# A Perceiver block on one core: key and value projections contract over 128 rows, 30 of them zero

## What is computed

```python
x = x + L0_xattn(layernorm(x), ctx)   # 4 heads, top 32 of 6272 scores, FiLM, S4D by FFT, MLP
x = x + L0_attn(layernorm(x))         # gated global mix, cumsum, 3-tap convolution
x = x + L0_ffn(layernorm(x))          # 8 experts, top 2, one shared
x = x + L1_xattn(layernorm(x), ctx)   # 16 heads of 8, softmax over 6272
x = x + L1_attn(layernorm(x))         # causal, 16 heads
x = x + L1_ffn(layernorm(x))          # 8 experts, top 2
# L1_xattn:
kh = (kv @ Wk + bk)...                # the key projection of this case
vh = (kv @ Wv + bv)...                # the value projection of this case
```

## Time and profile before

| | |
|---|---|
| median of 3 runs | 322.18 us (321.97 to 328.8) |
| the profiled execution | 320.57 us |
| its span, first to last instruction | 318.8 us |
| mean granted TensorE clock | 0.855 |
| TensorE busy | 244.7 us (77%) |
| VectorE busy | 195.1 us (61%) |
| ScalarE busy | 146.7 us (46%) |
| GpSimd busy | 66.1 us (21%) |

### The profile page before, as it was taken

How to read it: one execution, slowest core, us unless ns; L and a number is a source line. 1 busy time by engine, 2 the same in 40 slices (tenths; PEclk the granted TensorE clock), 3 DMA queues, 4 the chain that set the end, 5 groups by cost and what they waited for, 6 DMA issues and landing times.

```text
span 318.8 us, 5155 instructions
## 1 busy us (share of the span) xinstructions
PE 244.7 (77%) x2021; PEld 149.7 (47%) x2042; DVE 195.1 (61%) x482; ACT 146.7 (46%) x234; POOL 66.1 (21%) x97
## 2 busy tenths in 40 slices
PE   1995852596998658959777988998998888784884
PEld 1342312485873323424554855665665556431422
DVE  3299997898925464435236567776776770224464
ACT  1788930883623425235236575465565556301030
POOL 4895897002000442430013000000000000000000
PEclk9999595776999575558999999999999999757599
DMA  7992001000077000000089999999999509000000
GB/s 203 281 384 93 1 0 31 38 2 0 2 296 296 0 0 0 0 3 0 2 105 124 101 131 122 107 122 123 105 109 120 59 19 373 9 0 0 0 2 4
DMA packets 3807, 26.84 MB, mean 84 GB/s; under 512 B 1212, under 2 KB 1405, under 8 KB 2184
## 3 DMA queue, kind: packets, MB, share of 16 engines
q1 hardware_dynamic: 3784, 26.52, 42.1%
HBM read 16.85 MB, written 0.03 MB: 53 GB/s over the span
## 4 chain that ended last, share of the span: by engine, by line
PE 31%; DVE 9%; issue 5%; ACT 4%; POOL 1%; DVEq 0%; POOLq 0%; ACTq 0%
PE B L1039 17%; PE A L1039 12%; DVE mx L930 3%; ACT probs L606 1%; PE B L1337 1%; ACT mid L597 1%; DVE moe_w L927 1%; ACT moe_w L588 0%; ACT L606 0%; DVE m L969 0%; DVE probs L970 0%; DVE s L973 0%; POOL ctxn L434 0%; POOL ctxn L436 0%; DVE probs L962 0%
## 5 line engine op out<-in xcount | busy, mean ns | idle before, releaser
L930 DVE TENSOR_REDUCE mx<-B 128x1 f32<-128x512 f32 (+1 forms) x104 | 65.1, 656 | 26.2 <-PE B L1039 22.1
L606 ACT ACTIVATE probs<-A 128x896 f32<-128x896 f32 x56 | 51.3, 918 | 37.1 <-PE A L1039 36.8
L343 POOL TENSOR_TENSOR rstd<-ve,mhalf 64x1 f32<-64x1 f32 x10 | 5.5, 546 | 206.0 <-DVE ve L639 204.6
L1039 PE MATMUL B<-probs,scores 128*32 128x128 f32 x736 | 34.0, 280 | 4.9 <-ACT mid L597 3.5
L1039 PE MATMUL A<-ctxT,qq 98*128 98x512 f32 (+1 forms) x52 | 27.4, 690 | 5.4 <-ACT scores L464 4.9
L1039 PE MATMUL B<-scores,moe_w 128*128 128x512 bf16 (+2 forms) x118 | 29.2, 344 | 2.7 <-DVE mx L930 1.0
L1039 PEld LDWEIGHTS B<-probs,scores 128*32 128x32 f32 x736 | 19.2, 109 | 11.4 <-ACT probs L606 6.7
L673 DVE MAX8 mid<-scores 128x8 f32<-128x128 f32 x98 | 19.4, 279 | 4.5 <-ACT scores L464 4.5
L1039 PE MATMUL A<-ctxT,blob_l 98*128 98x512 f32 (+1 forms) x26 | 19.4, 879 | 3.4 <-DVE probs L779 3.4
L1039 PEld LDWEIGHTS A<-ctxT,qq 98*128 98x128 f32 x52 | 11.5, 232 | 21.8 <-issue 11.4
L1039 PE MATMUL A<-moe_w 112*128 112x128 bf16 (+2 forms) x146 | 19.8, 281 | 0.8 <-DVE moe_w L927 0.7
(11 more groups left out here) (347 smaller groups left out, 395.0 us busy)
## 6 DMA issues: line engine op xcount, KB each, us to landing
ctxT<-scores SPq DMA_DIRECT2D x20, 196.0 KB, 7.3
ctxn<-in_ctxn SPq DMA_DIRECT2D x1, 2352.0 KB, 8.2
moe_w<-in_moe_w SPq DMA_DIRECT2D x1, 2304.0 KB, 8.2
ctxn<-in_moe_w SPq DMA_DIRECT2D x1, 2304.0 KB, 9.0
scores<-in_e_gu SPq DMA_DIRECT2D x1, 2048.0 KB, 8.5
ctxn<-scores SPq DMA_DIRECT2D x10, 196.0 KB, 7.3
moe_w<-scores SPq DMA_DIRECT2D x10, 196.0 KB, 6.9
ctxT<-in_ctxT SPq DMA_DIRECT2D x3, 588.0 KB
```

The source lines that it names most:

```text
L343: nc.gpsimd.tensor_tensor(rstd[:, :], ve[:, :], mhalf[0:T, :], ALU.pow).then_inc(S["rstd_ready"], 1)
L606: A_(probs[:, (n % RING) * 1024:(n % RING) * 1024 + w], A[:, 2 * (n % 2):2 * (n % 2) + 2, :].rearrange("p a b -> p (a b)")[:, 0:w], ACT.Ex ...
L930: V.tensor_reduce(mx[:, m, t:t + 1], bank[:, 0:SB0[t][1]], AX_X, ALU.max).then_inc(S["max_used"], 1)
L1039: return mm(out_, lhsT, rhs, start=start, stop=stop)
```

## The change

The transposed context and both weights are used with all 128 rows. Rows 98 to 127 of `ctxT` are loaded as zeros from a new array `pad` (30 x 6272 float32, 735 KB), after `blob_l` and ahead of the wait for the mask rows. `wk1` and `wv1` get 30 rows of zeros on the host; `blob_l` keeps its size. TensorE waits for the new load once, ahead of the first key projection. The scores of the first block still use 98 rows. TensorE's order, its number of matmuls and their columns stay; the other engines' programs stay too.

```diff
-          "wq1": (D, D), "rep_q": (P, KS), "wv1": (KA, V_ROW), "bq1": (D, 1), "scale1": (P, 1), "wo1": (P, D),
-          "mask_hs": (P, 2), "mask_m": (P, NP), "sel_o": (P, 4 * 9), "wk1": (KA, D), "wqT2": (D, D), "wkT2": (D, D), "wvT2": (D, D), "woT2": (D, D),
+          "wq1": (D, D), "rep_q": (P, KS), "wv1": (P, V_ROW), "bq1": (D, 1), "scale1": (P, 1), "wo1": (P, D),
+          "mask_hs": (P, 2), "mask_m": (P, NP), "sel_o": (P, 4 * 9), "wk1": (P, D), "wqT2": (D, D), "wkT2": (D, D), "wvT2": (D, D), "woT2": (D, D),
...
             sp.dma_start(blob["blob_l"][:, :], dram["blob_l"]).then_inc(S["ld_l"], 16)
+            sp.dma_start(ctxT[KA:P, :], dram["pad"]).then_inc(S["ld_pad"], 16)
             sp.wait_ge(S["mask_row"], 4)
             sp.dma_start(ctxn[:, :], dram["ctxn"]).then_inc(S["ld_ctx"], 16)
...
-                    last = one(v_bank(b)[:, i * V_ROW:(i + 1) * V_ROW], chunk_cols(ctxT[0:KA, :], c), W["wv1"])
+                    last = one(v_bank(b)[:, i * V_ROW:(i + 1) * V_ROW], chunk_cols(ctxT, c), W["wv1"])
...
-                    one(A[:, n % 2, 0:w], W["wk1"], ctxT[0:KA, s:s + w]).then_inc(S["k_ps"], 1)
+                    one(A[:, n % 2, 0:w], W["wk1"], ctxT[:, s:s + w]).then_inc(S["k_ps"], 1)
...
             pe.wait_ge(S["ld_l"], 16)
+            pe.wait_ge(S["ld_pad"], 16)
             project_keys("film")
...
+    for n in ("wk1", "wv1"):
+        w[n] = np.concatenate([w[n], np.zeros((P - KA, w[n].shape[1]), np.float32)], 0)
...
+    out["pad"] = np.zeros((P - KA, G), np.float32)
```

More of the change, by code:

```diff
@@ L97 @@
 tokT_ps tokT_sb norm_ready k_ps k_hi k_rest k_mid k_low
-ld_a ld_s ld_m ld_l ld_rows ld_gmask ld_tmask ld_ctx ld_dft ld_w1 ld_w2 ld_gu ld_down out_stored
+ld_a ld_s ld_m ld_l ld_pad ld_rows ld_gmask ld_tmask ld_ctx ld_dft ld_w1 ld_w2 ld_gu ld_down out_stored
 ones_ready var_ready rstd_ready mask_row
```

## The result

The changed kernel took 314.25 us in the median of 4 executions (310.82 to 317.66), the kernel before 322.25 beside it: ratio 0.967 (95% interval 0.961 to 0.973), 8.0 us faster. The forecast was 319.2, with a range of 316.4 to 323.3: the sign was right, the size was not, and the time lies outside the range. The ratios and their intervals leave out every execution more than 1.5% above the fastest of its kernel, so that 0.967 rests on the changed kernel's executions at 310.82 and 312.41 us alone; the medians are over all executions, and their ratio is 0.975.

The account below looks back on a forecast made before the run. The prediction took a serial chain with TensorE at half clock as the bound. Gains of 0.9, 1.95 and 0.2 summed to 3.05, taken as 3.0 us off 322.18: 319.2 us, range 316.4 to 323.3.

Parts of the forecast that it names:

- What bounds the kernel: From 104.9 to 145.8 us: a serial one-block chain with key projections, TensorE doing 29.5 us of work at half clock.
- The mechanism: Matmuls count for the clock by rows contracted: 64 too few, 98 marginal, 128 best; zeros should not matter.
- The first rival, nothing happens: Rows do not count for the clock, or zero rows add nothing: time 322.2 us, chance 0.27.
- The load: Zero rows loaded ahead of `ctxn` make it land 2.6 us later, before its first read: 0 on the path.
- The bound of 21 us: Even at eight times the load's estimated price, `ctxn` would land before it is read.
- First stretch: No clock fall at 104.9 us, so the eight `hT` matmuls at 106.84 run at full clock: gain 0.9 us.
- The bound of 3.1: Upper bound in us for the first stretch, if all of 106.84 to 113.1 ran at full clock.
- Second stretch and behind it: Projections from 124.43 us raise the clock near 128.8, gaining 1.95; router work before the expert matmuls gains 0.2.
- the median moves by the same: Whole kernel: the median, 1.6 us above the profiled execution, drops by the same gain, to 319.2 us.
- rival of a fall in the expert stage: The clock falls near 154 us among the experts instead, costing 3 us: 324.2 us, chance 0.10.

Follow-up runs that it names:

- load_only: Kernel before plus the load of the zero rows and the wait for it, all projections still over 98 rows: 322.72 us, ratio 0.998.
- after_tail_fill: Changed kernel plus two matmuls of ones where TensorE waits right behind the main loop: 312.23 us, ratio 0.973.
- after_again: Changed kernel without any edit, executed six more times: median 318.20 us, from 310.3 to 321.9.
- pad_random: Changed kernel with random numbers instead of zeros in the context's 30 added rows, the weights' added rows still zero: 320.82 us, ratio 0.989.
- before_tail_fill: Kernel before, projections over 98 rows, plus two matmuls of ones right behind the main loop: 316.63 us, ratio 0.983.
- before_delay: Kernel before plus one unused GpSimd operation of 1.1 us between value projections and main loop: 324.47 us, ratio 0.997.

## Why the prediction was right and wrong

**What bounds the kernel: right.** The chain with the key projections at half clock was the place, and TensorE's clock was the lever: the first expert matmul moved 4.3 us forward (forecast: from 140.85 to near 138, measured 136.53; 0.6 of it lies ahead of the chain), and each microsecond behind it moved with it up to the loop's end (4.2 us).

**The mechanism: right, its rule too coarse.** Keys alone carry the chain's gain, values and load none; bursts of 64 rows stayed slow and bursts of 96 and more rose. Calling 98 rows marginal was fair: their bursts rose, and the longest piece over 98 rows rose in none of six profiles. But 128 rows were not better than 98 or 112 in the bursts, only in the kernel, and there 112 rows did in the first stretch what 128 do and in the longest piece no more than 98; the order by rows that the prediction assumed is shown for this piece, and nothing here shows where it comes from. Filled with zeros or with random numbers, the padded rows gave chains of 40.8 and 40.7 us, so zeros count, as argued from the mostly zero operands.

**The first rival, nothing happens: fell.** The times (0.967 at first, 0.980 for the keys alone) and the clock of the stretch (0.70 against 0.50) exclude it. The Trainium skill, page "TensorE: Matmul & The Clock Gate", section "What's actually happening", goes by how busy the array is; bursts of 17.43 us without a gap over 32, 64 and 80 rows stayed at half clock here, so in these runs the measurement decides against that rule as it stands, while the rule in its table at the end, that few rows take the time of many, holds at equal clock: 17.43 us three times.

**The load: no cost, as forecast, at a wrong price.** The estimate by bytes was 2.6 us more until `ctxn` lands after its issue; it was 4.6, and 8.0 in load_only, with the pad itself landing 19.6 and 23.1 us after issue. The price did not go by bytes. The bound of 21 us covered it.

**First stretch: half the size.** Forecast 0.9, measured 1.7 (first key projection to `ut`, 25.1 to 23.4 us). `hT` gave the 0.87 it should. What the sum left out is how far the later fall reaches: it came at 107.7, so the projection behind `hT` still ran in part at full clock (1.50 us for 2.02), and the projection at 117.52 began at full clock, ahead of the fall at 117.9 (1.72 for 2.07). The clock was back at 111.1, not 115.1, and the four projection instructions at 111.12 took 1.98 us instead of 2.99, but that gave nothing: the wait for VectorE behind them grew from 3.41 to 4.42. The bound of 3.1 held.

**Second stretch and behind it: right.** Forecast 1.95 to the end of `glob` and 0.2 behind it, measured 2.1 (132.70 became 128.26, with `ut` at 121.47 and 119.17) and -0.1. The rise came at 124.7, 2.6 us into the projections of 122.13, a little sooner than the 3 to 5.6 taken from other rises (in after_tail_fill the six took 5.51 us, with a rise only at their end), and VectorE's step became the limit ahead of the last two projections (the wait of 0.22 us), as the sum allowed for; the clock fell again at 131.6, before the experts. Sum of the chain: 3.7 instead of 3.05. By this execution alone, 316.08 for the 317.6 that was forecast for its like, and 0.6 of the difference is the earlier start of the chain.

**The step that failed: "the median moves by the same".** The sum took everything behind the expert stage as fixed, with one time. It is not: the tail from the loop's end takes 45 us or 39.3, and the experts and values 1 to 3 us more in some executions. In the kernel before, the fall behind the loop was in the one profile, and the narrow lower end of its 55 executions (none under 319.65) suggests that a tail without it hardly occurs; the changed kernel had it in one of two profiles, and four of its ten executions took 312.41 or less, where a chain 3.7 us shorter than in a profile of 320.57 doesn't lead. The two of these in the first comparison have no trace, but their granted clocks, 0.889 and 0.894, are near the 0.894 of after_again with its good tail and above the 0.881 of the profiled one. The prediction looked for falls that the change could cause (its rival of a fall in the expert stage, which did come, in pad_random and after_tail_fill) and not for falls of before that it could remove, though the earlier trace rows held the row of one: 64-row matmuls at half clock from 278.73 on. At the 5.0 to 5.5 us that before_tail_fill and after_again give for it, it would have been a rival at some 314 us, where the time came out.

**What stays open.** Why the kernel before never met the good tail and the changed one did. A filler of two matmuls shows that the fall is the whole cost, a delay of 1.1 us that shifting the work does not avoid it in most executions, and nothing here shows what decides between two executions of one kernel. Whether pad_random's extra falls are its data or its draw is open too, and so is why the longest piece tells 112 rows from 128 when the bursts do not. Float32 matmuls alone were tried in the bursts.

## What to carry to other kernels

Where a chain's TensorE work is short and stands at half clock, look at the rows over which its matmuls contract: from 98 to 128 with zeros cost nothing here and took 3.7 us out of a chain of 44.6 (to 112 rows only 1.6), and constant-operand fillers in the gaps did as much. Look then at every other place where the clock falls, behind long loops above all: two filler matmuls there were worth 5 us of 322, about as much as the change under study. And where the clock falls at all, a forecast from one profiled execution has to carry each fall of it, seen or possible, as a case of its own, and a few executions of a kernel whose times spread by 3 to 4% do not settle a change of 2%.

## What the runs showed of the hardware

- Float32 bursts of TensorE over 32, 64 and 80 rows stayed at half clock for 17.43 us; bursts over 96, 98, 112 and 128 rows rose 3.9 to 7.0 us in, with zero operands as with random ones, with 32 columns of weights as with 128.
- One unchanged single-core kernel took from 310.3 to 321.9 us, with mean granted clocks of 0.894 and 0.851 at the ends of that; of the 5.8 us between its two profiles 5.5 lie in the tail, which ran at 0.58 in one and at 1.00 in the other.
- In the kernel, six projection instructions in a row saw the clock rise over 128 rows (six profiles) and not over 98 (six) or 112 (one).
- A wait of 1.1 us ahead of steady TensorE work was followed by a fall of 3.4 us at half clock and cost 2.8 in all in one profile (before_delay); that it caused the fall is not shown.
- A load of 735 KB over 30 partitions took 19 to 23 us to land, among other loads on the same queue, and put a later one of 2352 KB back by 4.4 to 8.0 us, with nobody waiting for either.
